# Gathering expert rows in quarters, turning them on VectorE, and one stream of quarters between bursts of 3, 3, 2, 2 scores

## What is computed

```python
xn = layernorm(x)
# layer 0
q = rope(xn @ wq); k = rope(xn @ wk); v = xn @ wv          # 32 heads of 16, 8 key/value heads
s = softmax(mask(q @ k.T / 4)) @ v @ wo
logits = xn @ W_gate + b_gate                              # 8 experts, the best 2 of each token
g = mean over the 2 chosen of relu(xn @ W_e[e] + b_e[e])
x = x + s * silu(g)
xn = layernorm(x)
# layer 1: a causal convolution over features with a kernel from a state space model, and a linear layer
K = ifft(c * (k00 - k01 * k10 / (1 + k11))).real           # 64 states, 512 taps
s = causal_conv(xn, K) + D * xn
g = xn @ (dequantised weight).T + bias
x = x + s * silu(g)
```

## Time and profile before

| | |
|---|---|
| median of 3 runs | 770.04 us (769.16 to 782.33) |
| the profiled execution | 770.19 us, its span 768.4 us |
| mean granted clock of TensorE | 0.911 of 2.4 GHz |
| PE / PEld busy | 684.0 us (89%) / 382.1 us (50%) |
| DVE busy | 539.4 us (70%) |
| ACT busy | 302.2 us (39%) |
| POOL busy | 258.5 us (34%) |
| stage a ends, first transpose of maxima | 110.9 us |
| groups 3 to 30 | about 170 to 626 us |
| layer 1's first matmul | 678.74 us |

### The profile page before, as it was taken

How to read it: one execution, slowest core, us unless ns; L and a number is a source line. 1 busy time by engine, 2 the same in 40 slices (tenths; PEclk the granted TensorE clock), 3 DMA queues, 4 the chain that set the end, 5 groups by cost and what they waited for, 6 DMA issues and landing times. The chain is left out here.

```text
span 768.4 us, 12464 instructions
## 1 busy us (share of the span) xinstructions
PE 684.0 (89%) x3615; PEld 382.1 (50%) x3615; DVE 539.4 (70%) x1751; ACT 302.2 (39%) x555; POOL 258.5 (34%) x441
## 2 busy tenths in 40 slices
PE   3999966659899999999999999889899996769997
PEld 2788843334344444444434444444344442358886
DVE  4699887786675666777666776666677772458994
ACT  4344303323344444354344443344344450234542
POOL 2765526522232222223222222231122216146630
PEclk9999975567999999998999989799998997879999
DMA  6487869820635425146163241634515129337851
GB/s 226 134 280 263 262 161 263 191 48 23 110 91 124 85 64 104 56 78 112 50 131 73 48 91 43 118 70 91 88 32 93 56 77 291 87 82 184 215 136 70
DMA packets 52814, 92.26 MB, mean 120 GB/s; under 512 B 7800, under 2 KB 20664, under 8 KB 52752
## 3 DMA queue, kind: packets, MB, share of 16 engines
q1 hardware_dynamic: 40242, 63.95, 34.1%
q0 software_dynamic: 6704, 18.62, 11.1%
q10 hardware_dynamic: 5806, 8.94, 4.0%
HBM read 61.53 MB, written 29.43 MB: 118 GB/s over the span
## 5 line engine op out<-in xcount | busy, mean ns | idle before, releaser
L1207 DVE CUSTOM_DVE_ANT_0 bank<-bank,cst 128x384 f32<-128x384 f32 (+3 forms) x512 | 236.6, 521 | 112.5 <-PE bank L1386 109.2
L1306 ACT ACTIVATE arena<-bank 128x512 f32<-128x512 f32 x320 | 175.3, 601 | 130.7 <-PE bank L1408 114.2
L1076 POOL TENSOR_SCALAR_AFFINE_SELECT arena<-arena 128x512 f32<-128x512 f32 x128 | 85.6, 669 | 354.3 <-ACT arena L1306 354.1
L1466 PE MATMUL bank<-w_e,arena 128*128 x312 | 167.1, 648 | 0.0
L1386 PE MATMUL bank<-kt,qt 48*128 48x384 f32 (+3 forms) x512 | 135.0, 369 | 13.0 <-DVE arena L1207 11.5
L1386 PEld LDWEIGHTS bank<-kt,qt 48*128 48x128 f32 x512 | 82.0, 209 | 106.5 <-DVE arena L1207 56.5
L1408 PE MATMUL bank<-qt,kt 50*128 50x512 f32 x256 | 111.2, 526 | 16.1 <-DMA qt<-arena 13.8
L1436 PE MATMUL bank<-arena 128*32 128x512 f32 (+3 forms) x1024 | 90.8, 475 | 0.0
L1466 PEld LDWEIGHTS bank<-w_e,arena 128*128 128x128 f32 x312 | 55.8, 202 | 59.4 <-issue 56.7
L1207 DVE DVE_READ_ACCUMULATOR2_ANT arena<- 128x1 f32 x512 | 71.6, 140 | 0.0
L1479 PE MATMUL bank<-w_proj,arena 128*128 128x512 f32 x128 | 63.8, 631 | 6.7 <-DVE arena L630 5.8
(11 more groups left out here) (165 smaller groups left out, 993.8 us busy)
## 6 DMA issues: line engine op xcount, KB each, us to landing
qt<-turned_parts SPq DMA_DIRECT2D x96, 128.0 KB, 5.8
turned_parts<-qk_parts SPq DMA_DIRECT2D x8, 1280.0 KB, 6.7
expert_rows<-arena SPq DMA_DIRECT2D x39, 256.0 KB, 2.0
w_e<-in_L_ffn_W_e ACTq DMA_DIRECT2D x8, 1024.0 KB, 9.3
kt<-turned_parts SPq DMA_DIRECT2D x96, 64.0 KB, 5.2
arena<-in_L_attn_x SPq DMA_DIRECT2D x16, 256.0 KB, 3.6
xn_rows<-arena SPq DMA_DIRECT2D x16, 256.0 KB, 2.7
w_e<-in_L_attn_x SPq DMA_DIRECT2D x16, 256.0 KB, 3.7
```

Of the source, the lines that this page charges most:

```text
L1076: g.affine_select(out=diag, in_=diag, compare_op=ALU.is_ge, fill=0.0, base=0, pattern=[[0, 2], [0, HALF], [1, P]], channel_multiplier=-1). ...
L1207: i = v.tensor_tensor_reduce(out=part, in0=part, in1=const("mask")[:, S - w:], scale=1.0, scalar=LOWEST, op0=ALU.add, op1=ALU.max, accum_o ...
L1306: a.activation(pt[:, s, first:second + 1:second - first].rearrange("p c r q -> p c (r q)"), bank[2 + s].rearrange("p (c x) -> p c x", c=2) ...
L1466: i = t.matmul(bank[7], xgt[:, k, :], w_e[:, ex[b * MPB + m], k, :], start=False, stop=(k == KB - 1))
```

## The change

It touches stage `b` in four ways.

1. **Gathers.** The tokens' rows are read as four quarters of 512 bytes. For each tile POOL issues four indirect DMAs, one per block of 32 tokens; partition p takes quarter p // 32 of token 32 n + p % 32. The index lists are made once: `pe_tokens` (16 small matmuls into bank 7) and `dve_slots` (three operations), in group 2. Index copies are gone. The experts' weights are loaded with the rows of a partition contiguous to match.
2. **Turning.** One VectorE transpose of 32 x 32 blocks (`expert_x`) replaces four matmul transposes and ScalarE's copy. Bank 6 goes free and becomes the third bank of the second scores. When a tile is turned follows from the plan (`TURNS`): in a first slot, between maxima 7 and 8, or a second, after the group's finish. POOL gathers the tile two on in the same slot: the first lies between the masks of key blocks 2 and 3, the second after the last mask. Each gather waits until VectorE has turned the tile that held the buffer.
3. **Bursts.** Second scores go 3, 3, 2, 2 with S1 of the next group 2 pieces ahead, so that pieces 0 and 1 of the group after next are scored and measured in this group. Block order of masks and values is 0, 2, 3, 1, and pairs of blocks are formed anew.
4. **Quarters.** Experts and projections are one list of units, cut into quarters and dealt to five gaps per group: eight (2,2,1,1,2) in even groups, six (2,1,1,1,1) in odd ones; batch 0 has none in groups 0 to 2 and eight from group 3 on. The taps move behind the second of the last four projections, into bank 5.

By the plan, first slots are used in groups 3 to 7 of batch 0 and in 1, 3, 4, 5, 6, 7 of the others; second slots in 2, 3 (two tiles), 4, 5, 6 of batch 0 and in 2, 3, 5, 6 of the others.

```diff
+QUARTERS = [[(0,) * GAPS] * 3 + [(0, 2, 2, 2, 2)] + [(2, 2, 1, 1, 2)] * 4,
+            [(2, 2, 1, 1, 2), (2, 1, 1, 1, 1)] * 4,
+            [(2, 2, 1, 1, 2), (2, 1, 1, 1, 1)] * 4,
+            [(2, 2, 1, 1, 2), (2, 1, 1, 1, 1)] * 3 + [(2, 2, 1, 1, 2), (2, 0, 0, 0, 0)]]
...
+        def dve_slots(e, st):
+            v = nc.vector
+            e.wait_ge(r_turned, 1)
+            quarters = compared[:, 0:KB * MT]
+            v.tensor_scalar(quarters, bank[7][:, P:P + KB * MT], float(KB), None, ALU.mult).then_inc(dve_steps, st.one())
+            e.wait_ge(dve_steps, st.count())
+            v.tensor_scalar(quarters, quarters, const("quarter"), None, ALU.add).then_inc(dve_steps, st.one())
+            e.wait_ge(dve_steps, st.count())
+            v.tensor_copy(slots_i.rearrange("p t m -> p (t m)"), quarters).then_inc(r_slot_rows, 1)
+        def pe_tokens(e):
+            t = nc.tensor
+            e.wait_ge(r_tokens, 1)
+            for n in range(KB):
+                for k in range(KB):
+                    i = t.matmul(bank[7][32 * k:32 * (k + 1), P + n * MT:P + (n + 1) * MT], ident[:, 32 * n:32 * (n + 1)],
+                                 eid_f, start=True, stop=True, skip_group_check=True)
+            i.then_inc(r_turned, 1)
...
-            def gather(b, m):
-                if due(at := b * (8 * MPB) + 16 * (m // 2)):
-                    e.wait_ge(m_x[m % 2], at)
-                alone(e)
-                g.tensor_copy(tok_b[:, m % 2], slots_i[:, bass.ds(b * MPB + m, 1)]).then_inc(m_idx, 1)
-                if due(at := b * MPB + (m - 1)):
-                    e.wait_ge(m_xt, at)
-                e.wait_ge(m_idx, b * MPB + (m + 1))
-                alone(e)
-                e.indirect_dma_start(xg[:, m % 2, :], None, xn_d, bass.IndirectOffsetOnAxis(ap=tok_b[:, m % 2, :], axis=0))\
-                 .then_inc(m_x[m % 2], 16)
+            def gather(m):
+                if m > 1:
+                    e.wait_ge(m_xt, m - 1)
+                else:
+                    for u in range(TPB):
+                        e.wait_ge(a_store[u], 16 * NB)
+                    e.wait_ge(r_slot_rows, 1)
+                alone(e)
+                for n in range(KB):
+                    e.indirect_dma_start(xg[m % 2][:, n * P:(n + 1) * P], None, xn_q,
+                                         bass.IndirectOffsetOnAxis(ap=slots_i[:, n, m:m + 1], axis=0)).then_inc(m_x[m % 2], 16)
...
+            def go(b):                                      # POOL
...
+                    select(b, h, 0)
+                    select(b, h, 2)
+                    for m in TURNS.get((b, h, 0), ()):
+                        if m + 2 < MT:
+                            gather(m + 2)
+                    select(b, h, 3)
+                    select(b, h, 1)
...
+                    for m in TURNS.get((b, h, 1), ()):
+                        if m + 2 < MT:
+                            gather(m + 2)
...
+            def expert_x(m):                                # VectorE
+                e.wait_ge(m_x[m % 2], 16 * KB * (m // 2 + 1))
+                if m > 1:
+                    e.wait_ge(m_y, m - 1)
+                v.transpose(xgt[:, m % 2].rearrange("p (c t r) -> p t c r", t=KB, c=KB), xg[m % 2].rearrange("p (t k c) -> p t c k", t=KB, c=KB))\
+                    .then_inc(m_xt, 1)
...
+                    scores(e, (2, 3, 4), following, (0, 1, 2), (b, h))      # TensorE
+                    quarters(b, h, 0)
+                    scores(e, (5, 6, 7), following, (3, 4, 5), (b, h))
+                    quarters(b, h, 1)
+                    scores(e, (8, 9), following, (6, 7), (b, h))
+                    values(b, h, 0)
+                    quarters(b, h, 2)
+                    if (b, h) == (0, 2):
+                        pe_tokens(e)
+                    if following:
+                        turn_maxima(e, *following)
+                    scores(e, (0, 1), after, (8, 9), (b, h))
+                    quarters(b, h, 3)
+                    for j in ORDER[1:]:
+                        values(b, h, j)
+                    quarters(b, h, 4)
...
+                for k in range(KB):
+                    project(NB - 1, u, k, 7 - u % 2)
+                if u == 1:
+                    pe_taps(e)
```

More of the change, by code:

```diff
@@ L51 @@
 for _name, _n in (("ident", P), ("mask", S), ("tri", P), ("cos", TPB * 8), ("sin", TPB * 8), ("s4", 16),
-                  ("lower", E * E), ("i128", NT), ("i128m", MT + 1), ("tile", MT), ("iota", P), ("tilenum", TOPK * NT), ("part", 1), ("half", 1), ("eps", 1), ("minus", 1), ("sel", E)):
+                  ("lower", E * E), ("i128", NT), ("i128m", MT + 1), ("tile", MT), ("iota", P), ("tilenum", TOPK * NT), ("part", 1), ("half", 1), ("eps", 1), ("minus", 1), ("sel", E), ("quarter", 1)):
     COLS[_name] = (_at, _at + _n)
@@ L627, in dve_taps @@
             v.memset(taps[:, 0:P], 0.0).then_inc(dve_steps, st.one())
[L628 removed]
+            v.tensor_copy(taps[:, P:P + D], bank[5]).then_inc(dve_steps, st.one())
             e.wait_ge(dve_steps, st.count())
@@ L1339, in go @@
-                    if h + 1 < NG or more:
-                        maximum_rows(e, *next_group(b, h, 1), 1)
-                    if late:
-                        expert_y(b, first)
-                    if h < TPB and due(b):
-                        projected(e, b - 1, h)
-                    if second is not None:
-                        expert_y(b, second)
+                    if (b, h) == (0, 0):
+                        e.wait_ge(r_count, 1)
+                        a.copy(pos.rearrange("p t e -> p (t e)"), bank[7][:, 0:P])
+                        a.copy(tot.rearrange("p t e -> p (t e)"), bank[7][:, P:2 * P]).then_inc(r_copied, 1)
@@ L1348, in act_b @@
+                    for n in (8, 9):
+                        exps(b, h, n)
+                    results(b, h, 3, 4)
             for par in range(2):
@@ L1480, in project, with quarters, go @@
                 if k == KB - 1:
                     i.then_inc(b_p, 1)
+            def quarters(b, h, gap):
+                for n, k in WORK[b, h, gap]:
+                    kind, at = UNITS[n]
+                    if k == 0:
+                        bank_free(n)
+                    if kind == "x":
+                        expert(at, k)
+                    else:
+                        project(at // TPB, at % TPB, k)
             ex = {}
-            def go(b, more):
+            def go(b):
```

394 lines of the change are left out of this document (189 added, 205 removed).

## The result

The kernel before took 769.6 us in this comparison (median of 4 runs, 768.57 to 782.33), the changed one 779.21 (4 runs, 778.25 to 780.02). The ratio is 1.0129, 95% interval 1.0109 to 1.0149: slower by 1.3%. The run of 782.33 us is a slow execution of the kernel before and is not in the ratio. Forecast were 747 us, 3% faster, and a range of 714 to 772, so the time lies outside the range, though within 2% of the kernel before. The profiled execution's span is 776.4 us against 768.4.

A forecast was written before the change was run, and what follows sets the result against it. TensorE's stream paced the kernel before; after the change POOL's gathers ahead of the masks decide. Terms -0.6, -9.6, -5.8, -2, -8 and +3 sum to -23, from 770.04 to 747 us; range 714 to 772.

The forecast's parts named there:

- first rival: POOL's gathers hold the masks, four DMAs taking 4.6 to 5.3 us: 747 us, between 732 and 758; chance 0.5.
- G: Time four indirect DMAs of one gather hold POOL: 4.2 to 5.5 us, taken as 5.0.
- 1.94 + 6.4: First-slot group: the previous gap's quarters, 1.94 us, then 6.4 from the group's start through VectorE's turn.
- The turn, 0.71: VectorE's transpose of a gathered tile, priced at 0.71 us from its SBUF transpose; 39 of them, 28 us.
- 15.3: Forecast period in us of a group with only a first-slot gather: 10.3 + G.
- 122.4: Forecast length in us of a full batch: two groups each of 15.3, 13.6, 15.8 and 16.5.
- Stretch by stretch: Batches after batch 0: first -0.6 us against 123.05, second -9.6 against 131.98, last -5.8 against 95.92.
- Batch 0: Batch 0 from 169.76 us on: earlier routing end against later gathers and two back to back; -2 us taken.
- The end: Last transpose to second layer: taps moved behind two projections, 45 us for 52.85, so -8 us.
- Clock: Half-rate stretches of TensorE's clock after waits near 2 us, added as +3 us.
- Second rival: POOL passes the gathers quickly, under 4.2 us; TensorE's stream and stack loads bound, 110.8 a batch: 706 to 716; chance 0.18.

The follow-up runs named there:

- e1: The changed kernel with first-slot gathers issued behind the masks of key blocks 3 and 1: 725.21 us, ratio 0.9397 to the kernel before.
- e4: The changed kernel with VectorE's turn reading contiguous elements and the experts' weights loaded to match, four DMAs per expert: 770.48 us, ratio 0.9993.
- e16: The changed kernel unaltered, run again on a chip with prompt signals: 773.09 us, ratio 1.0054 to the kernel before.
- e17: The changed kernel with masks first, contiguous turn, and tile 0's turn and tile 5's gather moved later in batch 0: 715.7 us, ratio 0.9326.
- e7: e1 with the taps put back ahead of the last values, on a chip with late signals: 774.84 us, ratio 0.9976.
- e14: The same kernel as e7, run again on a chip with late signals: 775.98 us, ratio 1.0032.
- e2: The changed kernel issuing only one of each gather's four DMAs from the third tile on, in the old place: 723.92 us, one run.
- e11: e1 with only one of each gather's four DMAs from the third tile on: 709.92 us, ratio 0.9209.
- e9: e1's kernel unaltered, run again on a chip with prompt signals: 724.91 us, ratio 0.9405.
- e5: The changed kernel with both edits, masks first and contiguous turn, on a chip with late signals: 765.07 us, ratio 0.9844.
- e8: The changed kernel unaltered, run again on the chip of e5: 778.84 us, ratio 1.0038.
- e12: The changed kernel unaltered, run once more on a chip with late signals: 778.49 us, ratio 1.011.
- e15: The same kernel as e11, on a chip where four DMAs made signals late: 709.34 us, two runs, ratio 0.9194.
- e18: e1 with two of each gather's four DMAs from the third tile on, signals prompt: 711.15 us, two runs, ratio 0.9255.

## Why the prediction was wrong

The mechanism was the forecast's first rival, and e1 shows it: POOL held the masks, and TensorE's values waited some 1.6 us for them, as forecast. What failed is the length of what stands in front of the masks, from the start of VectorE's turn to the end of the gather: 0.71 + 5.0 us in the forecast, 1.11 + 0.75 + 4.7 measured. The second batch's lower clock and the late signals in batch 0 came on top.

- **G.** The four DMAs were priced at 5.0 and took 4.7: four of 0.95 and three gaps of 0.30. The gap that one pair had shown stands between all of them. But where the gather waits for VectorE's turn, the first DMA starts 0.75 behind it, and from the turn's end to the masks it is 5.45. The sum has no such term there: the group shown above reached its turn's end 8.8 us behind the values of the group before, where the forecast had 1.94 + 6.4, so only the 0.4 of the next point is missing up to there, and in the second slot the sum leaves 0.1 us for it. This handover was put at nothing. It comes in six of the ten gathers of the first full batch. The other four find their turn done and start 0.16 behind the masks, 4.86 in all. That is 6 x 0.45 - 4 x 0.14 = 2.1 us in the batch.
- **The turn, 0.71.** It was sized by transposes whose source is contiguous, although the diff reads every fourth element. It measured 1.11, and 0.70 without the stride (e4). This term had no upper bound in the prediction; that is the step that failed outright. It lengthens the same six gathers' groups by 0.4 each, 2.4 us. Together the two make the group with a first-slot gather alone 15.3 + 0.45 + 0.4 = 16.15 us, measured 16.37 and 16.45 in the first full batch, from the end of one group's last values to the next, and the batch 122.4 + 2.1 + 2.4 = 126.9, measured 127.3 and, on the prompt chip, 128.7. So the structure was right.
- **Stretch by stretch**, measured minus before, forecast in brackets: first batch +4.3 (-0.6), second +2.6 (-9.6), last -0.6 (-5.8). The two terms are worth 4.5, 4.5 and, with four gathers that wait and two that do not, 3.1, and the forecasts become +3.9, -5.1 and -2.7. So they account for the first batch, and for less than half of the second's miss. The second has besides one group of 21.4 us and a lower clock, which the sum did not have. In that group one gather has a gap of 2.24 us between its first two DMAs (the second starts at 492.15), with no wait that the trace can name; the trace of e16 has the same gap at 487.11.
- **Batch 0: +8.4 (-2).** e16 has 5.3 us less of it, so half of this miss is late signals, which the trace of the kernel before could not show. The rest, 5.1, is about what the two terms would give there, though that was not measured apart. A wait of the scores behind the turn of tile 0 (6.7 us in e1, 4.8 in e17) and one of the masks behind two gathers in a row (4.4 in e1, none in e17) were both there; the forecast had the second alone.
- **The end: -6.7 (-8).** Right but for 1.3 us; e7 and e14 show the taps' share as 5.
- **Clock: +3.** The first full batch ran at 1.00 of the granted clock and lost nothing. The second ran at 0.94, and TensorE was busy 114.73 us in it against 107.82 for the same instructions: 6.9 us, more than the 3 for all stretches.
- **Second rival (706 to 716).** With one DMA in the old place the time is 724, not 706 (e2): the full batch is 115 us, not 110.8. But with one DMA behind the masks it is 709.9, with full batches of 112.9 (e11), inside this rival's range. So it had the floor nearly right; its condition, a POOL that passes the four quickly, is what was not so. Between e2 and e11 TensorE's wait for the finished maxima ahead of their transpose (L1495) falls from 25.4 to 17.4 us, its wait of the first scores does not (15.8 and 16.5). Why the place matters even for one DMA was not followed up; e2 is one run.
- **The Trainium skill**, "DMA: Bandwidth & Descriptors", section "Anatomy of one DMA — SWDGE (gpsimd) path", calls the descriptors' generation small. The row of L1188 speaks against it: 0.954 us of POOL for each, with rows of 512 bytes little less than with the 2 KB rows of before (0.97 at least, 1.06 on the mean).

The sum of the misses on the span: 10.4 + 4.9 + 12.2 + 5.2 + 1.3, less the 3 for the clock, is 31.0, from the forecast 745.4 to 776.4.

There is something the forecast did not ask: it priced the gather's place and took it as given. The same DMAs two lines further down take 48 us less (773.1 in e16, 724.9 in e9, both with prompt signals).

## What to carry over

When one queued instruction becomes four, look first at what stands behind them in that engine's queue: move the waited-for work ahead before counting microseconds. An operation with a new access pattern has no row in the trace of before, however familiar its name; give it an upper bound of its own. And where two comparisons of one program disagree by 6%, look at the time from a producer's end to its consumer's start, before explaining either.

## What the runs showed of the hardware

- An indirect DMA of 128 rows holds POOL 0.95 us with rows of 512 bytes and 1.06 with 2 KB, and successive ones start 1.25 us apart even where nothing is waited for, with one gap of 2.24 instead of 0.30 in the second batch of the changed kernel. Where the first of four waited for a VectorE operation, it started 0.74 to 0.77 us behind its end.
- VectorE's 32x32 transpose of 128x512 fp32 takes 0.70 us from contiguous elements and 1.11 with every fourth element (e4 and the changed kernel).
- Around four indirect DMAs in a row VectorE and ScalarE can start 2 to 3.6 us behind the TensorE work that they wait for. The two chips of e5 to e8 and e12 to e15 showed it for the kernels with four, and the comparison of the result had it in batch 0; the chips of e1 to e4, e9 to e11 and e16 to e18 did not. One DMA did not cause it on the chip of e15. Its cause was not found.
- In e4 TensorE's clock fell behind a wait of 1.59 us (0.76 in the window behind it, four quarters in 3.09 us). In the changed kernel the same wait at 365.72 had a granted clock of 1.00 from 365 to 373 us.
